# A graph network in one kernel: setup steps of the counting stage moved into its own block and onto other engines, and every second quarter of the first attention turned round

## The reference

```python
q = jnp.einsum('nd,hdk->nhk', x, Wq) + bq        # layer 0, k and v alike, 4 heads of 64
scores = jnp.sum(q[dst] * k[src], axis=-1) / 8
alpha = softmax of scores over the edges of each dst
agg = segment_sum(alpha[:, :, None] * v[src], dst)
h = (agg + skip) @ Wout + bout + x                # then a layer norm
al_src = jnp.einsum('nhd,hd->nh', x1 @ W, a_src)  # layer 1: e = leaky_relu(al_src[src] + al_dst[dst])
```

## Time and profile before

| | |
|---|---|
| median of 3 runs | 4048.44 us (4046.75 to 4051.8) |
| profiled execution, its own time | 4048.74 us |
| its span, first to last instruction | 4047.0 us |
| TensorE busy, products | 3779.3 us (93%) |
| TensorE busy, weight loads | 2883.8 us (71%) |
| VectorE busy | 2334.7 us (58%) |
| ScalarE busy | 2057.9 us (51%) |
| GpSimd busy | 460.0 us (11%) |
| mean granted TensorE clock | 0.976 |
| first one-hot operation (end of the setup) | 60.44 us |
| counting ends, first attention's first product | 527.7, 549.2 us |
| first attention's last score | 1659 us |

### The profile page before, as it was taken

One profiled execution on the slowest core, in us unless ns is written; L12 is line 12 of the kernel. 1 busy time (PEld: TensorE's weight loads), 2 busy tenths in 40 slices (PEclk: granted clock), 3 DMA queues, 4 the chain that ended last, 5 costly groups with the idle time before them and its releaser, 6 DMA issues. The chain is left out here.

```text
span 4047.0 us, 69966 instructions
## 1 busy us (share of the span) xinstructions
PE 3779.3 (93%) x27513; PEld 2883.8 (71%) x27514; DVE 2334.7 (58%) x4672; ACT 2057.9 (51%) x3697; POOL 460.0 (11%) x594
## 2 busy tenths in 40 slices
PE   4999969999999999679998988979999999999999
PEld 2656536666666666457777777768888888888888
DVE  7999935555555565289999899810012221004665
ACT  1555536666666666479998788810001000003554
POOL 0000000111111111100003455410000000000000
PEclk9999979999999999889999999989999999999999
DMA  1555572233233323153342232243333333333342
GB/s 53 234 202 234 205 239 98 90 107 107 87 105 96 103 90 108 46 200 115 115 177 100 87 108 94 92 154 141 141 141 132 132 134 136 130 130 135 137 147 69
DMA packets 177168, 521.22 MB, mean 129 GB/s; under 512 B 54304, under 2 KB 141680, under 8 KB 143728
## 3 DMA queue, kind: packets, MB, share of 16 engines
q1 hardware_dynamic: 176096, 510.62, 35.7%
q10 hardware_dynamic: 784, 6.55, 0.6%
HBM read 354.82 MB, written 162.29 MB: 128 GB/s over the span
## 5 line engine op out<-in xcount | busy, mean ns | idle before, releaser
L1680 PE MATMUL t_acc<-t_r,t_ct 128*128 128x256 f32 (+1 forms) x3750 | 855.7, 380 | 18.5 <-DMA t_r<-d_r 15.2
L930 ACT ACTIVATE a_sm<-a_p_t 128x1024 f32<-128x1024 f32 (+1 forms) x800 | 669.9, 837 | 340.9 <-PE a_p_t L873 333.2
L887 PE MATMUL a_p_o<-a_sm,a_v 128*64 128x128 f32 x10000 | 746.8, 281 | 69.8 <-ACT a_sumT L937 69.7
L887 PEld LDWEIGHTS a_p_o<-a_sm,a_v 128*64 128x64 f32 x10000 | 554.1, 137 | 361.2 <-issue 201.8
L1680 PEld LDWEIGHTS t_acc<-t_r,t_ct 128*128 128x128 f32 x3750 | 701.2, 190 | 112.8 <-DMA t_r<-d_r 15.6
L873 PE MATMUL a_p_t<-ident,a_sm 128*128 128x128 f32 x5000 | 714.0, 281 | 50.4 <-ACT a_sm L924 33.2
L924 ACT ACTIVATE a_sm<-a_sm,a_negm 128x1024 f32<-128x1024 f32 (+1 forms) x600 | 707.1, 1178 | 72.9 <-DVE a_negm L990 72.6
L1010 DVE CUSTOM_DVE_ANT_0 a_sm<-a_p_s,a_full 128x400 f32<-128x400 f32 x800 | 428.1, 572 | 467.0 <-PE a_p_s L859 457.9
L873 PEld LDWEIGHTS a_p_t<-ident,a_sm 128*128 128x128 f32 x5000 | 562.9, 143 | 156.5 <-issue 133.8
L859 PE MATMUL a_p_s<-a_kt,a_q 64*128 64x400 f32 x1600 | 390.4, 560 | 34.5 <-DMA a_full<-d_logs 21.2
L1026 DVE SCALAR_TENSOR_TENSOR a_sm<-a_a_bc,a_al 128x3200 f32<-128x3200 f32 x100 | 354.2, 3542 | 50.2 <-PE a_p_o L887 25.8
(11 more groups left out here) (239 smaller groups left out, 3785.5 us busy)
## 6 DMA issues: line engine op xcount, KB each, us to landing
t_ct<-d_ct SPq DMA_DIRECT2D x74, 1600.0 KB, 6.7
a_mask<-d_full SPq DMA_DIRECT2D x50, 1600.0 KB, 7.0
d_logs<-logs SPq DMA_DIRECT2D x25, 1664.0 KB, 7.0
a_full<-d_logs SPq DMA_DIRECT2D x25, 1664.0 KB
d_ct<-ct SPq DMA_DIRECT2D x25, 1600.0 KB, 5.3
d_full<-a_full SPq DMA_DIRECT2D x25, 1600.0 KB, 5.6
t_ct<-d_full SPq DMA_DIRECT2D x25, 1600.0 KB, 6.9
a_a_bc<-d_as SPq DMA_DIRECT2D x8, 1600.0 KB, 10.3
```

The source lines that it names most:

```text
L887: m = nc.tensor.matmul(p_o[r:r + HD, 0:P], v[:, a, (p * heads + h) * HD:(p * heads + h + 1) * HD], sm[buf][:, a * P:(a + 1) * P], start=a ...
L930: nc.scalar.activation(sm[buf][:, a_row[u] * P:a_row[u + 1] * P], p_t[u % 2][:, 0:turns[u] * P], ACT.Copy).then_inc(s_copy, 1)
L1680: m = self.nc.tensor.matmul(self.acc[t % 2][:, 0:width], self.ct[t % 3][:, a * P:(a + 1) * P], rows[:, a, 0:width], start=a == 0, stop=a = ...
```

## The change

1. The identity is written by GpSimd at the head of the counting block, and the two earlier blocks are gone.
2. The attention vectors are made inside the counting block: the 14 loads are issued by ScalarE's queue, the zeros by GpSimd, the products by TensorE between its transposes, into p_t, and ScalarE copies them out.
3. The tables: GpSimd fills only their tails with -1, ScalarE copies the pieces from PSUM. VectorE waits for both just before the main loop.
4. VectorE makes src_low first, so that TensorE can start with it. The bounds take 7 operations and one reduction each for the first and for the last chunk, without waits among the 7. The scaling of iota_w comes after them.
5. In `attend` with dot=True TensorE runs quarters 1 and 3 in the reverse order: weigh, score, turn.

Cut to its core (left out: new names, semaphores and arguments, and `attention_vectors`, which is deleted whole):

```diff
@@ constants
-    s_ident = ctx.enter_context(nc.semaphore("s_ident"))
-    with nc.Block() as block:
...
@@ build_counts, gpsimd
+                pool.memset(ident[:, :], 0.0).then_inc(s_ident, 1)
+                pool.memset(a1[:, :, :], 0.0).then_inc(s_vzero, 1)
+                pool.wait_ge(s_ident, 1)
+                pool.affine_select(out=ident[:, :], in_=ident[:, :], compare_op=ALU.not_equal, fill=1.0,
+                                   base=0, pattern=[[-1, P]], channel_multiplier=1).then_inc(s_ident, 1)
                 pool.iota(iota_g[:, :], [[1, NG]], base=0, channel_multiplier=0, allow_small_or_imprecise_dtypes=True).then_inc(s_iota, 1)
...
+                for a in (low_t, key_t):
+                    for o in (0, ODD):
+                        pool.memset(a[:, o + CB * P:o + CW if o else CW + 1], -1.0).then_inc(s_tail, 1)
@@ build_counts, vector
-                v.memset(hi_p[:, :], 0.0)
-                v.memset(lo_p[:, :], 0.0)
-                link(v.memset(low_t[:, :], -1.0))
-                link(v.memset(key_t[:, :], -1.0))
                 dve.wait_ge(s_edges, 96)
...
+                for bound, edge, chunk, order in ((hi_p, first_g, chunk_after, ALU.is_ge), (lo_p, last_g, chunk_back, ALU.is_le)):
+                    for k in range(CB):
+                        last = v.tensor_scalar(reached[:, k, :], iota_g[:, :], edge[:, k:k + 1], chunk[:, k:k + 1], order, ALU.mult)
+                    link(last)
+                    link(v.tensor_reduce(bound[:, :], reached[:, :, :].rearrange("p k g -> p g k"), AX.X, ALU.max))
+                dve.sem_inc(s_bound, 1)
+
                 link(v.tensor_scalar(iota_w[:, :, :], iota_w[:, :, :], 0.5, None, ALU.mult))
-                for k in range(CB):
-                    link(v.tensor_scalar(at_least[:, :], iota_g[:, :], first_g[:, k:k + 1], None, ALU.is_ge))
-                    link(v.scalar_tensor_tensor(inside[:, :], iota_g[:, :], last_g[:, k:k + 1], at_least[:, :], ALU.is_le, ALU.mult))
-                    link(v.scalar_tensor_tensor(hi_p[:, :], inside[:, :], chunk_after[:, k:k + 1], hi_p[:, :], ALU.mult, ALU.max))
-                    link(v.scalar_tensor_tensor(lo_p[:, :], inside[:, :], chunk_back[:, k:k + 1], lo_p[:, :], ALU.mult, ALU.max))
...
-                    link(v.tensor_copy(to[:, half * UNIT:half * UNIT + w], p_e[:, half, 0:w]))
-                    link(v.tensor_copy(to[:, ODD + half * UNIT:ODD + half * UNIT + w], p_e[:, half, 0:w]))
...
+                dve.wait_ge(s_ecopy, 4)
+                dve.wait_ge(s_tail, 4)
@@ build_counts, tensor, behind the four pieces
+                pe.wait_ge(s_vin, 16 * (2 + 8 + 4))
+                for m in range(2):
+                    for c in range(2):
+                        nc.tensor.matmul(p_t[:, 0, m * 2 * H0:(m + 1) * 2 * H0], w1T[:, c, m * P:(m + 1) * P], a1[:, c, :], start=c == 0, stop=c == 1)
...
@@ build_counts, scalar, ahead of the rest
+                for a, d in ((w1T, w["w1T"]), (w3T, w["w3T"])):
+                    act.dma_start(a[:, :, :], d.rearrange("(c p) n -> p c n", p=P)).then_inc(s_vin, 16)
+                act.wait_ge(s_vzero, 1)
...
+                for n in range(2 * 2):
+                    act.wait_ge(s_ebank, n + 1)
+                    to, half = (low_t, key_t)[n // 2], n % 2
+                    m = UNIT if half == 0 else CB * P - UNIT
+                    for o in (0, ODD):
+                        copied = nc.scalar.activation(to[:, o + half * UNIT:o + half * UNIT + m], p_e[:, half, 0:m], ACT.Copy)
+                    copied.then_inc(s_ecopy, 1)
...
@@ attend, tensor, body
                     for u in range(ntu):
-                        if exists(at):
+                        turns_first = not dot or u % 2 == 0
+                        if turns_first and exists(at):
                             turn(at, u)
+                        if not turns_first and behind(at, 1) is not None:
+                            weigh(behind(at, 1), u)
                         if dot and u in SCORE_AT and ahead(at, 2) is not None:
                             score(ahead(at, 2), SCORE_AT[u])
-                        if behind(at, 1) is not None:
+                        if turns_first and behind(at, 1) is not None:
                             weigh(behind(at, 1), u)
+                        if not turns_first and exists(at):
+                            turn(at, u)
```

More of the change, by code:

```diff
@@ L212, in projection, with build_counts @@
     return Projection
-def build_counts(nc, src, dst, ident, ct_dram, log_dram, layer0):
+def build_counts(nc, src, dst, ident, ct_dram, log_dram, layer0, vectors):
     ctx = ExitStack()
@@ L265, in build_counts @@
         ct_own = sb("ct_own", [P, P], FP32)
+        w1T = sb("w1T", [P, 2, D], FP32)
+        w3T = sb("w3T", [P, 2, D], FP32)
+        a1 = sb("a1", [P, 2, 2 * H0], FP32)
+        a3 = sb("a3", [P, 2, 2], FP32)
         p_g = pb("p_g", [P, QUAD, UNIT])
@@ L272, in build_counts @@
         proj = projection(nc, sb, pb, sem, ident, layer0)
+        s_ident = sem("c_ident")
+        s_tail = sem("c_tables_filled")
+        s_vzero = sem("c_vectors_zero")
+        s_vin = sem("c_vectors_in")
+        s_vproduct = sem("c_vector_products")
+        s_vcopy = sem("c_vectors_copied")
         s_fill = sem("c_fill")
@@ L460, in _ @@
                     last.then_inc(s_ebank, 1)
+                pe.wait_ge(s_vin, 16 * (2 + 8 + 4))
+                for m in range(2):
+                    for c in range(2):
+                        nc.tensor.matmul(p_t[:, 0, m * 2 * H0:(m + 1) * 2 * H0], w1T[:, c, m * P:(m + 1) * P], a1[:, c, :], start=c == 0, stop=c == 1)
+                    for c in range(2):
+                        last = nc.tensor.matmul(p_t[:, 1, m * 2:(m + 1) * 2], w3T[:, c, m * P:(m + 1) * P], a3[:, c, :], start=c == 0, stop=c == 1)
+                last.then_inc(s_vproduct, 1)
                 pe.wait_ge(s_bound, 1)
@@ L540, in _ @@
             def _(act):
+                w = vectors
+                for a, d in ((w1T, w["w1T"]), (w3T, w["w3T"])):
+                    act.dma_start(a[:, :, :], d.rearrange("(c p) n -> p c n", p=P)).then_inc(s_vin, 16)
+                act.wait_ge(s_vzero, 1)
+                for k, a in ((0, w["a_src1"]), (1, w["a_dst1"])):
+                    for h in range(H0):
+                        r = (h % 2) * HD
+                        act.dma_start(a1[r:r + HD, h // 2, k * H0 + h:k * H0 + h + 1], a[h:h + 1, :].rearrange("o k -> k o")).then_inc(s_vin, 16)
+                for k, a in ((0, w["a_src3"]), (1, w["a_dst3"])):
+                    for c in range(2):
+                        act.dma_start(a3[:, c, k:k + 1], a[c * P:(c + 1) * P].rearrange("(p o) -> p o", o=1)).then_inc(s_vin, 16)
+                for n in range(2 * 2):
[5 more added lines that the diff above has]
+                    copied.then_inc(s_ecopy, 1)
+                act.wait_ge(s_vproduct, 1)
+                nc.scalar.activation(w["wa1"][:, :, :], p_t[:, 0, 0:4 * H0].rearrange("p (m n) -> p m n", m=2), ACT.Copy).then_inc(s_vcopy, 1)
+                nc.scalar.activation(w["wa3"][:, :, :], p_t[:, 1, 0:4].rearrange("p (m n) -> p m n", m=2), ACT.Copy).then_inc(s_vcopy, 1)
                 act.wait_ge(s_tiny, 1)
```

76 lines of the change are left out of this document (14 added, 62 removed).

## The result

| | before | after |
|---|---|---|
| median of 5 runs each | 4051.80 us | 4018.13 us (4008.07 to 4023.65) |
| ratio, 95% interval | | 0.9916 (0.9905 to 0.9927) |
| profiled execution, its span | 4048.74, 4047.0 us | 4018.61, 4016.8 us |
| first one-hot operation | 60.44 us | 39.28 us |
| first attention, first to last score | 549.2 to 1659.4 us | 528.7 to 1622.1 us |

The change is faster by 0.84%, 33.7 us by the medians. Forecast were 87.7, and the range went from 3950 to 3988: the result lies outside. In the two profiled executions 30.2 us of span are gained: 21.2 at the end of the setup and 37.3 at the end of the first attention, of which the stages behind it give 7 back.

The account below looks back on a forecast made before the run. The prediction took VectorE's chain to bound the setup and TensorE the first attention. From 4048.7 us it took 27.8 for the setup and 59.7 for the attention, giving 3961 us, range 3950 to 3988.

Parts of the forecast that it names:

- (a): Setup: two blocks gone, edges asked for first; VectorE begins at 7.2 us instead of 25.35, 18.1 less.
- (b): Setup: the nine operations to last_g are the same work, 0 us gained.
- (e): Setup: table copies leave VectorE for ScalarE, hidden there; 4.4 us less between bounds and their reduction.
- (d): Setup, bounds: 14 operations and two reductions instead of 28 dependent operations, 4.9 us less, ends 0.3 and 5.6.
- (f): Setup: from the bounds' reduction to the first one-hot operation, 51.49 to 60.44 us, unchanged.
- The rival of ScalarE's late queue: Setup: ScalarE issues its loads slowly, the path runs over its copies, 11 us back, 3972 us; chance 0.05.
- The joints: First attention: four places per unit where like quarters adjoin save 0.15 us each, 0.61 per unit, 59.7 in all.
- dear: First attention: each weigh-to-score step costs 0.1 to 0.15 us more, 19 to 29 back, 3980 to 3990; chance 0.10.
- the joints save nothing: First attention: a semaphore wait at each quarter's start breaks the stream; setup alone gains, 4021 us; chance 0.06.
- Can the others follow?: First attention: VectorE and ScalarE keep up with TensorE; no wait or under 0.1 us, ScalarE with one us left.
- The rival on the clock: First attention: a denser TensorE is granted a lower clock; at 0.90 105 us more, 4066 us; chance 0.02.
- A wait that eats all: A wait in ScalarE's or VectorE's order, priced at nothing, uses up the whole gain; chance 0.02.

Follow-up runs that it names:

- e6: e3 with GpSimd's tail fills ahead of its iotas and the bounds laid out so the reduction reads without a stride: 3997.0 us, 0.9852 of before.
- e9: Changed kernel with e6's setup, source terms made turned by two extra products and stored in rows, GpSimd's tail fills held until the bounds: 3971.7 us.
- e4: Changed kernel, source-term store replaced by 8 packets of 512 bytes from another tile, so later attention has other numbers: 3964.0 us, 0.9767 of before.
- e7: Kernel before with e4's store of the source terms: 4046.2 us, 0.9988 of before.
- e1: Changed kernel with the quarters back in their old order, so the setup alone: 4036.7 us, 0.9959 of before.
- e2: Kernel before with only quarters 1 and 3 reversed: 4021.3 us, 0.9925 of before.
- e3: Changed kernel with TensorE's transposes of a finished tile (L1303) one quarter later: 3991.1 us, 0.9854 of before.

## Why the prediction was wrong, by its steps

**(a) Blocks gone.** VectorE began at 8.67 us, not 7.2: 1.5 us less than priced, within its ends. From the first request to VectorE's start are 7.9 us, between the 6.5 that were priced and the 9.3 of the end in which the weights take their share.

**(b) "The same work, 0".** Wrong: the first operation took 2.45 us more. (e) had cleared GpSimd's fills, since they are done in time; that they stand beside VectorE's first operation was not asked. e6 and e9 show the cost. The Trainium skill has the rule in "SBUF — State Buffer", Who interferes with whom: a tensor_scalar of VectorE can run in a mode that needs the pair of SBUF ports it shares with GpSimd, and whichever of the two comes second is blocked until the other's instruction ends. The traces agree: 0.63 us alone, 3.08 and 3.27 beside GpSimd, and in the changed kernel it stayed blocked over several fills. By that rule the step would have cost what GpSimd had left to do.

**(c)** 0.37 us moved, as said. **(d) Bounds.** From 18.80 to 28.5 us is 9.7, not 7.3: the strided reduction 2.63 instead of 1.7, the seven operations 2.15 instead of 1.9. The ends (0.3 to 5.6 us gained) held, at 2.5. **(e)** 1.3 us from bounds to their reduction, 1.4 were predicted, and the copies and products were hidden. **(f)** 9.5 instead of 8.95. Sum: 21.2 us instead of 27.8; the 6.6 missing are 1.5 + 2.45 + 2.4 + 0.5, less 0.1 gained in (e), within the rounding. The rival of ScalarE's late queue fell: its issues were done at 9.1 us.

**The joints.** Right, in mechanism and size. A plain unit takes 9.83 us (forecast 9.86), and weigh to score adds nothing, so the rivals "dear" and "the joints save nothing" fall. In e4 the stage saves 66.6 us, for 59.7: the joints give 0.65 per unit instead of 0.61, the tiles' other units 0.68, and some 3 us lie in the first tile, as in e7.

**"Can the others follow?"** This step failed, and with it the forecast: it put TensorE's waits for the others at nothing or under 0.1 us per unit, and they and what follows them took some 48 us of the stage. It followed ScalarE through a plain unit, where "one us is left", and took TensorE's releases as punctual. In a tile's unit with the w1 product ScalarE has the values to read as well, and TensorE's L1303 waits for them. From the release of quarter 1's turn to the end of the values is 4.8 us of ScalarE (1357.60 to 1362.37 above: copy, exponential, copy, exponential, values). Before, the turn started at 956.48, so the values could be ready at 956.48 + 1.13 + 4.8 = 962.4 and were wanted at 965.02: 2.6 us of slack. In e4 the same turn starts at 958.23, and the values are wanted at 964.34: 0.2 us left. (Against a late turn of quarter 2 the kernel before had less, 0.8 us, but that turn came 11 us behind the store, when most releases were punctual again.) The new order used 2.4 us of slack that the kernel had against late releases. Late releases were there in both, but the new order also meets more of them: the copy of this turn started over 1.4 us after the turn in 20 of 25 tiles of the changed kernel's profile, at most 3.9 us late, and in 8 before, at most 1.7 late. e1 has 9 such tiles and e2 18, so it is the order. In it the turn stands 8.2 us behind the store in the middle tile, not 7.4; that this is why is not shown.

**What each part took.** Against e4's tiles the changed kernel's units are 48 us longer in sum, 41 of them in the units with L1303. The wait for the values is 30.1 us over the whole stage (22 times, 2.2 us at the longest). Part of the rest is what follows a long wait: at 1362.96 eight transposes took 1.91 us instead of 1.04 and the weigh behind them 3.08 instead of 1.97. From the fourth tile to the end of the stage the clock stood at 0.5 for 20 us, in five stretches, which can explain 10; about 8 us are in neither. So the clock is a consequence here. The rival on the clock was wrong about its cause, since e4 is denser still and has 1.00. Two of the signs that the prediction named did show: ScalarE as releaser ahead of TensorE's work, and a clock of 0.99 instead of 1.00 between 600 and 1500 us; a plain unit gave neither away. "A wait that eats all", given 0.02, was the right kind of rival, with far too little chance and no place.

**What stays open.** Why packets of 4 bytes, which the trace has finished 2 to 4 us after the store is asked for in most tiles, make TensorE's releases late 7 to 14 us after it. Only that they do is shown: by taking them away in both kernels, and by doubling them. The Trainium skill, "DMA: Bandwidth & Descriptors", Specifications, says that transfers under 512 bytes are read, modified and written back, and so run below the full rate; no run here shows that mechanism. The medians of e3 and e6 differ by 6 us, of which 3 are in those of before beside them; the rest is not explained. Of the 7 us that the stages behind the first attention gave back in the profile of the changed kernel, 5 lie 504 to 1036 us behind the last score, where the clock stood at its lower level for 75 us instead of 65; why is not shown.

## What to carry to other kernels

A tighter order on the busiest engine spends slack of the others. Follow the waiting chain through the fullest unit of the loop, not the plain one, and compare what is left with how late releases already are in the trace of before: there the start of a copy behind its turn varied by microseconds at no cost, and that was the warning. A store that writes 4 bytes at a time cost nothing in the loop while there was slack, and 35 to 48 us when it was gone; turn the tile on TensorE, beside other transposes, and store rows.

## What the runs showed of the hardware that was not expected

- A store of 1,024 packets of 4 bytes per tile: TensorE's releases come up to 4 us late, 7 to 14 us after the store is asked for (8 packets of 512 bytes: none late). Two such stores: up to 7 us late, mostly 8 to 18 us after them, and the kernel before becomes 3.1% slower.
- VectorE's tensor_scalar on 128x896 int32: 0.63 us alone, 3.08 and 3.27 beside a memset or an iota of GpSimd, until GpSimd's work was done; on 128x800 f16 0.37 and 1.82.
- A reduction of 1,400 elements: 1.61 us in order, 2.63 with a stride of 200 elements. Writing the input with a stride of 7 instead cost 0.08 for seven operations.
- Two products of 128 columns between a product and a turn: 0.68 us. One transpose between transposes: 0.11.
